# A graph and expert layer on one core: the experts' two layers pipelined over steps, and three of seven tail tiles summed on TensorE

## What is computed

```
h  = layernorm(x) @ W_gat;  e = leaky_relu(a_src[src] + a_dst[dst])
agg = segment_softmax_sum(e, h[src], dst) + b_gat
scores = layernorm(agg).reshape(M, HEADS, 4).mean(1);  top 2 of 4, w = softmax(top 2)
for ei in range(4):
    g  = where(topk_i == ei, w, 0).sum(-1)
    hh = gelu(xn @ W1[ei] + b1[ei])          # 256 -> 512
    out += g[..., None] * (hh @ W2[ei] + b2[ei])   # 512 -> 256
```

## Time and profile before

| | us |
|---|---|
| median of three runs | 3596.13 |
| the profiled execution | 3581.74 |
| its span | 3580.0 |
| stage2 with its experts, 28 steps (1822 to 3225) | 1403 |
| rest of stage2 (3225 to 3397) | 172 |
| carry of the last edges, and tail (3397 to 3580) | 183 |

### The profile page before, as it was taken

The page is one execution under the profiler, slowest core; times in us unless marked ns, Lnnn a source line. Parts: engine busy times, 40 slices in busy tenths (PEclk is TensorE's granted clock), DMA queues, the critical chain, the costliest instruction groups (busy, mean ns, idle before and its releaser), DMA issues. The chain is left out here.

```text
span 3580.0 us, 24262 instructions
## 1 busy us (share of the span) xinstructions
PE 1439.0 (40%) x4434; PEld 903.5 (25%) x4434; DVE 1826.5 (51%) x3777; ACT 1360.1 (38%) x3390; POOL 2186.9 (61%) x2136
## 2 busy tenths in 40 slices
PE   2556601221122212212516565666556666571012
PEld 2333400111111111102404332334233443241002
DVE  7677787888888878865732211112121221221138
ACT  1322256766677667752402222222222222131111
POOL 0543666776667766737666667566666666667750
PEclk8677855555555555555558777778777878785556
DMA  4412645665566656636331111111111111111166
GB/s 128 140 58 64 177 139 192 194 209 186 187 210 200 205 187 198 204 121 201 104 90 36 34 24 37 23 36 36 34 36 24 36 34 36 34 39 27 16 206 234
DMA packets 227596, 391.47 MB, mean 109 GB/s; under 512 B 53315, under 2 KB 184050, under 8 KB 220112
## 3 DMA queue, kind: packets, MB, share of 16 engines
q1 hardware_dynamic: 137556, 258.07, 20.7%
q0 software_dynamic: 80880, 124.27, 15.6%
q10 hardware_dynamic: 9100, 8.50, 0.7%
HBM read 201.15 MB, written 189.55 MB: 109 GB/s over the span
## 5 line engine op out<-in xcount | busy, mean ns | idle before, releaser
L1217 POOL DMA_INDIRECT stage_got<-ffn_rows,stage_idx x1024 | 1041.9, 1017 | 532.6 <-issue 327.8
L1217 POOL DMA_INDIRECT edges_got<-gnn_rows,edges_idx x728 | 730.0, 1003 | 337.1 <-issue 259.5
L2074 PE MATMUL stage_ph<-ffn_xt_all,stage_w 128*128 (+1 forms) x896 | 487.3, 685 | 461.7 <-ACT stage_hid L2109 209.0
L2132 DVE TENSOR_TENSOR search_found<-stage_po,stage_b 128x256 f32<-128x256 f32 x196 | 77.8, 422 | 1067.6 <-DMA x_again_X<-in_x_dram 418.7
L1296 DVE TENSOR_TENSOR_SCAN stage_y<-stage_decays,stage_y 128x960 f32<-128x960 f32 (+2 forms) x288 | 526.7, 1877 | 13.5 <-ACT stage_decays L1263 9.1
L2086 PE MATMUL stage_po<-stage_w,stage_hid 128*128 128x256 f32 x1568 | 378.4, 402 | 129.9 <-issue 84.4
L1257 ACT ACTIVATE stage_weights<-stage_chunk_parts 128x64 f32<-128x64 f32 (+1 forms) x120 | 28.9, 240 | 993.9 <-DVE stage_chunk_parts L1251 714.9
L2074 PEld LDWEIGHTS stage_ph<-ffn_xt_all,stage_w 128*128 128x128 f32 x896 | 210.3, 240 | 727.8 <-issue 450.6
L1318 ACT ACTIVATE stage_rows<-stage_y 128x896 f32<-128x896 f32 x224 | 372.7, 1819 | 9.9 <-issue 9.9
L2086 PEld LDWEIGHTS stage_po<-stage_w,stage_hid 128*128 128x128 f32 x1568 | 310.3, 201 | 204.8 <-issue 133.2
L1592 PE MATMUL stage_pm<-setup_ident,stage_mix_parts 128*128 128x128 f32 x98 | 32.4, 434 | 754.5 <-ACT stage_mix_parts L1618 347.8
(11 more groups left out here) (467 smaller groups left out, 2495.7 us busy)
## 6 DMA issues: line engine op xcount, KB each, us to landing
state_gnn<-stage_rows SPq DMA_DIRECT2D x56, 1848.0 KB
y<-search_found SPq DMA_DIRECT2D x28, 896.0 KB
tail_fin_y<-y SPq DMA_DIRECT2D x7, 3584.0 KB
stage_got<-ffn_rows,stage_idx POOLq DMA_INDIRECT x1024
edges_got<-gnn_rows,edges_idx POOLq DMA_INDIRECT x784
state_ffn<-stage_rows SPq DMA_DIRECT2D x64, 192.0 KB
mix_rows<-stage_mix_parts SPq DMA_DIRECT2D x49, 131.0 KB
x_again_mix<-mix_rows SPq DMA_DIRECT2D x7, 917.0 KB
```

Of the source, the lines that this page charges most:

```text
L1217: pool.indirect_dma_start(out=got[:, u, t, :], out_offset=None, in_=self.row_dram[g.name][:, :], in_offset=bass.IndirectOffsetOnAxis(ap=id ...
L2074: mm = pe.matmul(ph[:, n % 4, 0:HALF], w1[:, e, k, f * P:(f + 1) * P], xt_all[:, k, bass.ds(b * (B * P) + half * HALF, HALF)], start=(k == ...
```

## The change

In ffn_and_experts there are two hid buffers, used in turn; the second is the array seg of the start phase, and ACT waits once (room_free) until DVE's start work is over. PE computes all eight groups of step 0 first. Then, in step q, it waits for all gelus of q, computes groups 0 to 3 of step q+1, tiles 0 and 1 of q, and then group 4, tile 2, group 5, tile 3, group 6, tile 4, group 7, tiles 5 and 6. ACT's order is the same, but its wait before the gelus is for all tiles of step q-2. DVE handles chunks 0 and 1 first, and in step q chunk 2q+2, takes 0 to 2, chunk 2q+3, takes 3 to 6; SP's stores follow that order. PE and ACT loop over pairs of steps (walk_by_two), with single steps written out at the ends. In the tail, three tiles of a group of seven go by PE instead of two.

```diff
--- before.py
+++ after.py
@@ -948,7 +948,7 @@
         seg_loaded, last_ready, spread, chained, turned, ramps, carry_taken = (self.sem(mine, n) for n in names)
 
         class Steps:
-            done = carry_taken
+            done, room = carry_taken, seg[:, :, :].rearrange("p w c -> p (w c)")
 
             def pool_ramps(pool):
                 pool.iota(ramp_i, pattern=[[1, W]], base=-W, channel_multiplier=0)
@@ -1998,20 +1998,21 @@
             w1 = self.sb(here, "w1", [P, EXPERTS, 2, HIDDEN])
             w2 = self.sb(here, "w2", [P, EXPERTS, FT, D])
             b1, b2 = self.sb(here, "b1", [P, EXPERTS, FT]), self.sb(here, "b2", [P, EXPERTS, D])
-            hid = self.sb(here, "hid", [P, FT, B * P])
+            hid_even = self.sb(here, "hid", [P, FT, B * P])
             yrow = self.found[:, :].rearrange("p (t d) -> p t d", d=D)
             ph, po = self.ps(here, "ph", [P, 4, 512]), self.ps(here, "po", [P, 4, 512])
-            names = ("w_loaded", "hid_made", "hid_ready", "out_made", "out_used")
-            w_loaded, hid_made, hid_ready, out_made, out_used = (self.sem(here, n) for n in names)
+            names = ("w_loaded", "hid_made", "hid_ready", "out_made", "out_used", "room_free")
+            w_loaded, hid_made, hid_ready, out_made, out_used, room_free = (self.sem(here, n) for n in names)
             y_out = self.sem(here, "y_out")
             edge = self.chunk_parts(FFN, here, fin, finm, self.gather_parts(FFN, here, here))
             begun = self.starts_parts(FFN, here, po[:, 3, 0:P], po[:, 3, P:2 * P])
+            hid = (hid_even, begun.room[:, 0:FT * B * P].rearrange("p (f n) -> p f n", f=FT))
             by_tile = self.y_dram.rearrange("(t p) e d -> p t e d", p=P)
             block = here.enter_context(nc.Block())
 
-            def first_step(q, e):
-
-                return isinstance(q, int) and q == 0 and e == 0
+            def first_step(q):
+
+                return isinstance(q, int) and q == 0
 
             def walk(eng, step, rest):
 
@@ -2021,9 +2022,18 @@
                 for e in range(1, EXPERTS):
                     with eng.Fori(0, blocks) as b:
                         step(b, e, b + e * blocks)
-                if rest is not None:
-                    with eng.Fori(blocks * EXPERTS, pairs) as i:
-                        rest(i)
+                with eng.Fori(blocks * EXPERTS + 1, pairs) as i:
+                    rest(i)
+
+            def walk_by_two(eng, step):
+
+                for e in range(EXPERTS):
+                    for b in range(2 if e == 0 else 0):
+                        step(b, e, b, b % 2)
+                    with eng.Fori(1 if e == 0 else 0, blocks // 2) as n:
+                        for half in range(2):
+                            step(n * 2 + half, e, n * 2 + (half + e * blocks), (half + e) % 2)
+                    step(blocks - 1, e, blocks - 1 + e * blocks, (blocks - 1 + e) % 2)
 
             @block.gpsimd
             def _(pool):
@@ -2042,9 +2052,12 @@
                         sp.dma_start(b1[:, e, f:f + 1], io["L0_ffn_b1"][e, f * P:(f + 1) * P].rearrange("(p a) -> p a", a=1)) \
                           .then_inc(w_loaded, 16)
 
+                edge.sp_store(sp, 0, 0)
+                edge.sp_store(sp, 1, 1)
+
                 def step(b, e, q):
-                    edge.sp_store(sp, q * 2, 0)
-                    edge.sp_store(sp, q * 2 + 1, 1)
+                    edge.sp_store(sp, q * 2 + 2, 0)
+                    edge.sp_store(sp, q * 2 + 3, 1)
                     sp.wait_ge(out_used, q * B + B)
                     sp.dma_start(by_tile[:, bass.ds(b * B, B), e, :], yrow[:, :, :]).then_inc(y_out, 16)
 
@@ -2060,33 +2073,45 @@
             def _(pe):
                 pe.wait_ge(w_loaded, 16 * EXPERTS * (3 + FT))
 
-                def step(b, e, q):
+                def first_layer(b, e, q, n):
+                    f, half = n // 2, n % 2
+                    if not (first_step(q) and n < 4):
+                        pe.wait_ge(hid_ready, q * EH + (n - 3))
+                    for k in range(2):
+                        mm = pe.matmul(ph[:, n % 4, 0:HALF], w1[:, e, k, f * P:(f + 1) * P],
+                                       xt_all[:, k, bass.ds(b * (B * P) + half * HALF, HALF)],
+                                       start=(k == 0), stop=(k == 1))
+                    mm.then_inc(hid_made, 1)
+
+                def second_layer(e, q, s, t):
+                    slot = t % 4
+                    if t >= 4:
+                        pe.wait_ge(out_used, q * B + (t - 3))
+                    elif not first_step(q):
+                        pe.wait_ge(out_used, q * B + (t + 5 - B if t + 4 < B else t + 1 - B))
                     for f in range(FT):
-                        for half in range(2):
-                            n = f * 2 + half
-                            if first_step(q, e) and n == 4:
-                                begun.pe_last(pe)
-                                begun.pe_chain(pe)
-                                pe.wait_ge(begun.done, 1)
-                            if not (first_step(q, e) and n < 4):
-                                pe.wait_ge(hid_ready, q * EH + (n - 3))
-                            for k in range(2):
-                                mm = pe.matmul(ph[:, n % 4, 0:HALF], w1[:, e, k, f * P:(f + 1) * P],
-                                               xt_all[:, k, bass.ds(b * (B * P) + half * HALF, HALF)],
-                                               start=(k == 0), stop=(k == 1))
-                            mm.then_inc(hid_made, 1)
+                        mm = pe.matmul(po[:, slot, 0:D], hid[s][:, f, t * P:(t + 1) * P], w2[:, e, f, :],
+                                       start=(f == 0), stop=(f == FT - 1))
+                    mm.then_inc(out_made, 1)
+
+                def step(b, e, q, s):
+                    last = isinstance(b, int) and b == blocks - 1
+                    ahead = (0, e + 1) if last else (b + 1, e)
+                    more = ahead[1] < EXPERTS
                     pe.wait_ge(hid_ready, q * EH + EH)
+                    for n in range(4 if more else 0):
+                        first_layer(*ahead, q + 1, n)
                     for t in range(B):
-                        slot = t % 4
-                        if t >= 4:
-                            pe.wait_ge(out_used, q * B + (t - 3))
-                        elif not first_step(q, e):
-                            pe.wait_ge(out_used, q * B + (t + 5 - B if t + 4 < B else t + 1 - B))
-                        for f in range(FT):
-                            mm = pe.matmul(po[:, slot, 0:D], hid[:, f, t * P:(t + 1) * P], w2[:, e, f, :],
-                                           start=(f == 0), stop=(f == FT - 1))
-                        mm.then_inc(out_made, 1)
-                walk(pe, step, None)
+                        second_layer(e, q, s, t)
+                        if more and 1 <= t < 5:
+                            first_layer(*ahead, q + 1, t + 3)
+                for n in range(EH):
+                    if n == 4:
+                        begun.pe_last(pe)
+                        begun.pe_chain(pe)
+                        pe.wait_ge(begun.done, 1)
+                    first_layer(0, 0, 0, n)
+                walk_by_two(pe, step)
 
             @block.scalar
             def _(act):
@@ -2098,22 +2123,25 @@
                     edge.act_exps(act, c, s)
                     edge.act_rows(act, c, i, s)
 
-                def step(b, e, q):
+                def step(b, e, q, s):
                     chunk(q * 2, q, 0)
-                    if not first_step(q, e):
-                        act.wait_ge(out_made, q * B)
-                    for f in range(FT):
-                        for half in range(2):
-                            n = f * 2 + half
-                            act.wait_ge(hid_made, q * EH + (n + 1))
-                            act.activation(hid[:, f, half * HALF:(half + 1) * HALF], ph[:, n % 4, 0:HALF],
-                                           ACT.Gelu, bias=b1[:, e, f:f + 1]).then_inc(hid_ready, 1)
+                    if isinstance(q, int) and q == 1:
+                        act.wait_ge(room_free, 1)
+                    if not (isinstance(q, int) and q < 2):
+                        act.wait_ge(out_made, (q - 1) * B)
+                    for n in range(EH):
+                        f, half = n // 2, n % 2
+                        act.wait_ge(hid_made, q * EH + (n + 1))
+                        act.activation(hid[s][:, f, half * HALF:(half + 1) * HALF], ph[:, n % 4, 0:HALF],
+                                       ACT.Gelu, bias=b1[:, e, f:f + 1]).then_inc(hid_ready, 1)
                     chunk(q * 2 + 1, q, 1)
 
                 def rest(i):
                     chunk(i * 2, i, 0)
                     chunk(i * 2 + 1, i, 1)
-                walk(act, step, rest)
+                walk_by_two(act, step)
+                with act.Fori(blocks * EXPERTS, pairs) as i:
```

(13 more changed lines are left out.)

## The result

| | kernel before | changed kernel |
|---|---|---|
| median of 20 runs each, same chip, us | 3596.66 (3576.54 to 3616.1) | 3571.3 (3555.89 to 3587.41) |
| ratio | | 0.9929, 95% interval 0.9912 to 0.9945 |
| profiled execution and its span, us | 3581.7, 3580.0 | 3561.48, 3559.8 |
| POOL's waits for indices in stage2 | 204.0 us, 25 times | 181.5 us, 23 times |
| stage2 from first gather to the end of the last | 1573.7 us | 1552.6 us |

The change is worth 25 us in the medians. It makes the kernel faster, as forecast, by well under half of the 66 us, and the time lies between the forecast's 3530 and the 3590 of rival (B).

The account below looks back on a forecast made before the run. POOL was taken to bound stage2, with only its 204.0 us of waits for indices removable. Terms -78.4 + 18 - 6 = -66 us, from the median 3596.1, gave 3530 us; range 3450 to 3625, the forecast's own 3481 to 3571.

Parts of the forecast that it names:

- rival (B): Stage2: what TensorE completes while POOL gathers is scarce whatever the order; stops stay 204 us, only the tail gains: 3590; chance 0.15.
- The bound: Stage2: POOL is the chain, 1041.9 us of gathers and 327.8 between them; only its 204.0 us of waits can go.
- The lag: Stage2 and tail: while POOL gathers without a break, TensorE's completions come up to 40 us late, arriving when POOL stops.
- (1), the short stops: New order on PE in stage2: POOL's 13 stops of 3.08 to 6.81 us go, -78.4 us; bounds 0 and -78.4.
- (2), the long stops: Stage2, new wait on PE: POOL's 12 stops of 7.66 to 19.91 us grow by 1.5 each, +18; bounds 0 and 84.
- Group 4's new wait: On PE: group 4 waits for the next step's first gelu, with tiles 2 to 6 and groups 5 to 7 queued behind.
- (3) to (5): Two hidden buffers, DVE's chunks a pair ahead with SP's stores, loops over two steps: all taken to cost nothing.
- (6), the tail: Three of seven tiles on PE: -1.3 us a group, five groups gain, group 0 loses 0.4: -6 us; bounds -9 and -2.
- (A): Stage2: the lag goes altogether with shorter PE bursts and POOL never stops, -204.0 - 6, giving 3386; chance 0.13 with halfway cases.
- (D): Stage2, slower: tile 2's late take holds DVE's odd chunk, POOL stops 10.3 us after every chunk pair; 3674 or 3632; chance 0.15.
- (C): Stage2: new waits keep TensorE at its lower clock, 1.2 GHz, PE becomes the bound, 20 us saved, 3570; chance 0.05.

## Why the prediction came out so

**The bound.** Right. POOL's gathers and issue are a floor of 1369 to 1371 us in stage2, reached to the microsecond on chip 1, and what lies above it are the waits for indices.

**The lag.** Right as a mechanism, and shown: ACT and PE both idle for over 20 us with every matmul issued, and on time with a break of POOL in each chunk. That it belongs to some chips (or to their state at the time) and not to others was not foreseen.

**(1), the short stops: the step that failed.** I took the short stop as gone, -78.4 us, since the take of tile 2 comes earlier (right: it no longer holds the chunk) and the last gelu, with 5.3 us more of PE ahead of it, was covered by ACT's 10.89 us of idle time. I counted this 5.3 us as bare work of PE, with no lag on it, one paragraph after finding completions up to 40 us late. By moving group 7 behind tile 4, the change made the last gelu wait for a completion deep in PE's queue, and it comes 25 us late. The cover was under half of that. The short stop of 6.8 us became one of 7.7 us on another chain. The sums over stage2, idle time of every cause, show the same shift: DVE's ahead of the takes fell from 1068 to 351 us, and ACT's ahead of the gelus rose from 173 to 840.

**(2), the long stops.** I took 12 of them to grow by 1.5 us each, +18. Instead most long stops of 10 us gave way to ones of 7.7, since the chain behind the late completion is now ACT's 4.1 us rather than three takes and a whole DVE chunk; three stops of 13 to 14 us were left. Terms (1) and (2) together were -60 and measured -22.5 us of waits: twice 7.7 where there were 10.0 and 6.8. Group 4's new wait itself hardly showed: in the step above its gelu is one of the four of 2458.02, and PE idles 0.36 us.

**(3) to (5).** At nothing, and right within some 3 us as far as can be seen: the pipelining alone costs 3.2 us on chip 1.

**(6), the tail.** -6 forecast, -6.7 between the traces and -5.1 alone on chip 1. Group 0 late by POOL's last gather and group 3 held by PE, both as worked out.

**The rivals.** (A), no stop at all, needs a pause of POOL, and then the pause costs the same. (B) lies nearer than the forecast: its 3590 is 19 us above the result, the forecast 41 below, and the result is at the very edge of the forecast's own range. Its mechanism is supported, not shown, by three runs: two orders that leave the sum of the waits at 210 to 217 us, and less work for TensorE that lowers it. It is not the whole truth: all tiles first raised the sum to 270.7, so an order can be worse, and in both of the other orders another late completion stood in the odd chunk's way, so that no run had an order free of them. (D) had the right pattern, a stop after every pair of chunks, through a chain that it didn't name and with 7.7 us where it put 10.3; at 10.3 the change would have been a loss. (C) did not occur: the granted clock was 0.75, and PE was busy 780.6 of 1400.4 us, far from being the bound. The rule on bursts of matmuls with idle time between them (the Trainium skill, TensorE: Matmul & The Clock Gate, section "HAM oscillation — how this bites in real kernels") agrees with the traces in that the clock was 0.75 with such gaps and 0.96 in the run with PE busy 689 of 750 us; that it had no say in the time is argued from POOL being the bound.

**What stays open.** Why gathers hold completions back on chips 0 and 9 and not on 1 and 3; each of the late chips was used in one set of runs, so the chip and its state then can't be told apart. Whether other work of POOL does the same: the run with one gather in sixteen, meant for this, fell on a prompt chip. Whether fewer or shorter breaks would win; that the breaks cost just what the stops did may be chance. All timed runs were profiled, so whether the lag exists without the profiler can't be told. No version with the whole computation clearly beat the changed kernel on a late chip; on chip 1 the tail alone has the lowest time, 3175.38 us, with the 3176.68 of groups 4 to 7 in one row within its interval.

## What to carry to other kernels

Once a trace shows completions to come late, every wait on that engine has to be priced with the lag, those that an edit moves deeper into its queue above all; idle time that covered the old wait covers nothing then. Where a stop of the bounding engine is itself what lets the late completions through, reordering the others can move the stop rather than remove it, as every order tried here did, and its length is the chain behind the last completion: shorten that chain, or give the engine less to complete. And compare one kernel on more than one chip before optimising against a wait: here the wait was worth 200 us in this stage on two chips and nothing on two others.

## What the runs showed of the hardware

- One kernel took 3597 us on two chips and 3180 to 3184 us on two others. Of the some 415 us, about 200 are POOL's waits for indices in stage2 (1573.7 us with the earlier trace rows, 1369 us on chip 1); another 188 come ahead of stage2, which starts at 1822.0 us in the earlier trace rows and at 1633.8 us in the tail's run on chip 1, and no run here takes them apart.
- On the two slower chips, while POOL issues indirect gathers 0.30 us apart, the end of a matmul is seen by the waiting engine up to 26 us late in the rows above (2346.3, the profile's modelled end of group 4 in the kernel with all tiles first, to 2372.32), and within 5 us of the start of POOL's last gather (2367.7 to 2372.32; 2490.47 to 2495.01). A pause of POOL that costs 3.1 us on the mean (197 us in 64 breaks) in every 16 gathers was enough to have the gelus on time (281 us of idle time ahead of them, 283 on chip 1).
- A drain of POOL between two gathers costs 2.9 us by itself (183 us in 64, chip 3 against chip 1).
